# The last FFN stage with half of its tokens sorted by expert through DRAM

## What is computed

```
x = x + 0.5 * _L1_ffn_ref(_layernorm(x), ...)
shared = silu(xf @ shared_w1.T) * (xf @ shared_w2.T) @ shared_w3.T
scores = sigmoid(xf @ router_w.T)
_, top_idx = top_k(scores + expert_bias, 2)
gates = scores * one_hot(top_idx, 8).sum(-2)
h = silu(h1) * h2 * gates[:, :, None]        # h1, h2 of all 8 experts
routed = einsum('teh,edh->td', h, w3)
```

## Time and profile before

| | us |
|---|---|
| runs | 730.72, 729.73, 727.52 (median 729.73) |
| span of the profiled execution, first to last instruction | 725.0 |
| its own time | not among the three runs shown |
| PE busy | 676.2 (93%) |
| DVE busy | 570.1 (79%) |
| ACT busy | 419.2 (58%) |
| POOL busy | 325.0 (45%) |

### The profile page before, as it was taken

How to read it: one execution, slowest core, us unless ns; L and a number is a source line. 1 busy time by engine, 2 the same in 40 slices (tenths; PEclk the granted TensorE clock), 3 DMA queues, 4 the chain that set the end, 5 groups by cost and what they waited for, 6 DMA issues and landing times. The chain is left out here.

```text
span 725.0 us, 12469 instructions
## 1 busy us (share of the span) xinstructions
PE 676.2 (93%) x4100; PEld 505.7 (70%) x4100; DVE 570.1 (79%) x1308; ACT 419.2 (58%) x757; POOL 325.0 (45%) x404
## 2 busy tenths in 40 slices
PE   6899998797879999999999888999999997999997
PEld 5677774643457777777778676777777775777785
DVE  5799977899968888988989856666766675889774
ACT  4567686885245555556655657555565654555553
POOL 2668883201227766465658461220413200555463
PEclk9999999999999999999999989999999999999999
DMA  6625520000013232222222000000000000323141
GB/s 168 201 99 177 173 72 1 0 1 1 1 40 137 70 106 89 87 61 83 94 58 90 29 1 2 1 2 1 2 1 0 0 2 3 116 71 120 55 122 43
DMA packets 34329, 43.16 MB, mean 60 GB/s; under 512 B 5216, under 2 KB 17504, under 8 KB 34272
## 3 DMA queue, kind: packets, MB, share of 16 engines
q1 hardware_dynamic: 34272, 42.46, 18.9%
HBM read 41.13 MB, written 1.31 MB: 59 GB/s over the span
## 5 line engine op out<-in xcount | busy, mean ns | idle before, releaser
L698 POOL TENSOR_TENSOR p_prod<-p_p,p_gate_row 128x512 f32<-128x512 f32 x128 | 203.9, 1604 | 106.9 <-DVE p_p L505 62.4
L385 ACT ACTIVATE p_sil<-p_ps_a 128x512 f32<-128x512 f32 x176 | 105.3, 598 | 131.4 <-PE p_ps_a L100 128.3
L510 DVE TENSOR_TENSOR p_hlo<-p_prod,p_hhi 128x512 fp32r<-128x512 f32 x176 | 150.3, 855 | 0.3 <-ACT p_hhi L394 0.2
L505 DVE TENSOR_TENSOR p_p<-p_sil,p_ps_b 128x512 f32<-128x512 f32 x128 | 87.1, 681 | 52.6 <-ACT p_sil L385 38.1
L394 ACT CAST p_hhi<-p_prod 128x512 fp32r<-128x512 f32 x176 | 108.1, 615 | 23.0 <-POOL p_prod L698 22.9
L98 PE MATMUL p_ps_a<-xt_hi,w_uphi 128*128 128x512 f32 x176 | 74.2, 422 | 0.0
L98 PE MATMUL p_ps_acc<-p_hhi,w_downhi 128*128 128x512 f32 x176 | 71.1, 404 | 1.2 <-DVE p_hlo L510 1.0
L98 PE MATMUL p_ps_b<-xt_hi,w_uphi 128*128 128x512 f32 x176 | 71.0, 404 | 0.2
L99 PE MATMUL p_ps_a<-xt_lo,w_uphi 128*128 128x512 f32 x176 | 70.1, 399 | 0.0
L100 PE MATMUL p_ps_a<-xt_hi,w_uplo 128*128 128x512 f32 x176 | 70.1, 398 | 0.0
L100 PE MATMUL p_ps_b<-xt_hi,w_uplo 128*128 128x512 f32 x176 | 70.0, 398 | 0.0
(11 more groups left out here) (355 smaller groups left out, 1425.1 us busy)
## 6 DMA issues: line engine op xcount, KB each, us to landing
p_gate_row<-gate_rows SPq DMA_DIRECT2D x128, 256.0 KB, 3.3
w_rawbuf<-in_L_ffn_fc_w_dram SPq DMA_DIRECT2D x3, 512.0 KB, 7.1
w_rawbuf<-in_L_ffn_w_dram SPq DMA_DIRECT2D x3, 512.0 KB, 6.1
out_dram<-x SPq DMA_DIRECT2D x4, 256.0 KB, 3.6
w_rawbuf<-in_L_ffn_shared_w_dram SPq DMA_DIRECT2D x3, 256.0 KB, 5.6
x<-in_L_attn_x_dram SPq DMA_DIRECT2D x2, 256.0 KB, 3.9
x<-in_L_attn_x_dram SPq DMA_DIRECT2D x1, 512.0 KB, 9.3
mb_xraw<-in_L_attn_W_B_dram SPq DMA_DIRECT2D x1, 512.0 KB, 4.8
```

Source lines behind the costliest of these rows:

```text
L385: nc.scalar.activation(sil[:, u % 2], ps_a[:, u % 2], ACT.Silu).then_inc(c["sil"].sem, 1)
L505: nc.vector.tensor_tensor(dst, sil[:, u % 2], ps_b[:, u % 2], ALU.mult).then_inc(c["p1"].sem, 1)
L510: nc.vector.tensor_tensor(hlo[:, u % R], prod[:, u % R], hhi[:, u % R].bitcast(F32), ALU.subtract).then_inc(c["hlo"].sem, 1)
L698: G.tensor_tensor(prod[:, u % R], p1[:, u % 2], gate_row[:, e % ROWS], ALU.mult).then_inc(c["prod"].sem, 1)
```

## The change

Blocks 0 and 1 of the last stage (1024 tokens) keep only their 4 shared units; their 8 expert units go. Blocks 2 and 3 stay dense with 12 units. So the stream (`sparse_stream`) has 4 + 4 + 12 + 12 = 32 units for 48. For the 1024 tokens the kernel instead:

1. routes both blocks at the start (`z_route`, `z_choose`), counts with 9 small matmuls (`z_rank`) where each of the 2048 (token, expert) pairs stands in a list sorted by expert, each expert padded to whole tiles: 23 slot tiles at most (`z_places`),
2. scatters each normalised token to its two slots in DRAM: 16 indirect DMAs on POOL,
3. in six groups of four slot tiles (the last of three), between unit 15 and unit 16: loads the rows, turns them, and multiplies each tile with the weights of its own expert alone, which a register read from SBUF picks (`value_load`, 23 times on PE),
4. stores the results in DRAM, fetches each token's two rows with 16 indirect DMAs on POOL, and adds them, weighed by the gate, on DVE (`z_add`).

In block 3 the gate is multiplied by DVE and no longer by POOL. The slots are zeroed beforehand by one DMA of 128 x 23 x 128 numbers, put ahead of `load_rest`. Mamba keeps the normalised tokens of both blocks (one copy per block on POOL, `save_head`).

The diff, cut to its core:

```diff
+def three_pass_turned(pe, out, tokens, weights):
+    pe.matmul(out, tokens[0], weights[0], start=True, stop=False)
+    pe.matmul(out, tokens[0], weights[1], start=False, stop=False)
+    return pe.matmul(out, tokens[1], weights[0], start=False, stop=True)
...
+                G.memset(consts["zeros"], 0.0)
...
+def sparse_stream(nc, tag, counts, sb, ps, x, xt, consts, kind, gate_dram, rows_dram, results_dram, norm, kept_xn, le, tail, out_dram, room, spent_zs, spent_raw):
+    LEAD, BEHIND, RING, ROWS = 4, 2, 4, EXPERTS
+    S, U, w = kind.shared, kind.units, kind.w
+    FIRST = (0, S, 2 * S, 2 * S + U)
+    UNITS = 2 * S + 2 * U
+    CUT = 16
+    GROUPS = -(-SLOT_TILES // BT)
+    HALF = 2 * BT
+    STRIDE = P
...
+        @block.tensor
+        def _(pe):
...
+            def z_rank():
+                pe.wait_ge(c["z_both"].sem, c["z_both"].at(1))
+                pe.matmul(ranks, le[:], z_both[:], start=True, stop=False)
+                for j in range(1, HALF + 1):
+                    last = pe.matmul(ranks[:, j:], z_ones[:], z_both[:, 0:HALF + 1 - j], start=False, stop=j == HALF)
+                last.then_inc(c["z_rank"].sem, 1)
+            def z_owners(s):
+                if s == 0:
+                    pe.wait_ge(c["z_owner"].sem, c["z_owner"].at(1))
+                for q in range(s * BT, s * BT + sizes(s)):
+                    owner[q] = pe.value_load(z_owner[0:1, q:q + 1], min_val=0, max_val=(EXPERTS - 1) * STRIDE)
+            def z_turn_x(s):
+                row = c[f"z_row{s % 2}"]
+                pe.wait_ge(row.sem, row.at(16 * (s // 2 + 1)))
+                if s == 0:
+                    pe.wait_ge(c["gts"].sem, c["gts"].at(2))
+                else:
+                    pe.wait_ge(c["z_xlo"].sem, c["z_xlo"].at(s))
+                for t in range(sizes(s)):
+                    last = pe.transpose(ps_t[:, bass.ts(t, P)], z_rows[s % 2][:, t], ident[:])
+                last.then_inc(c["z_xt"].sem, 1)
+            def z_up(s):
+                if s < 2:
+                    before = c[("sil", "p1")[s]]
+                    pe.wait_ge(before.sem, before.at(CUT + LEAD))
+                else:
+                    pe.wait_ge(c["z_h"].sem, c["z_h"].at(s - 1))
+                pe.wait_ge(c["z_xlo"].sem, c["z_xlo"].at(s + 1))
+                for t in range(sizes(s)):
+                    some = bass.ds(owner[s * BT + t] * 2 + S * 2 * P, 2 * P)
+                    last = three_pass_turned(pe, raised(s)[:, t].rearrange("p a c -> p (a c)"),
+                                             [q[s % 2][:, bass.ts(t, P)] for q in (z_xhi, z_xlo)], [q[:, some] for q in up_flat])
+                last.then_inc(c["z_up"].sem, 1)
+            def z_turn_h(s):
+                pe.wait_ge(c["z_h"].sem, c["z_h"].at(s + 1))
+                if s:
+                    pe.wait_ge(c["z_hlo"].sem, c["z_hlo"].at(s))
+                else:
+                    pe.wait_ge(c["out"].sem, c["out"].at(2))
+                for t in range(sizes(s)):
+                    last = pe.transpose(ps_o[:, bass.ts(t, P)], z_h[s % 2][:, t], ident[:])
+                last.then_inc(c["z_ht"].sem, 1)
+            def z_down(s):
+                pe.wait_ge(c["z_hlo"].sem, c["z_hlo"].at(s + 1))
+                if s:
+                    pe.wait_ge(c["z_yc"].sem, c["z_yc"].at(s))
+                else:
+                    pe.wait_ge(c["lgs"].sem, c["lgs"].at(2))
+                for t in range(sizes(s)):
+                    some = bass.ds(owner[s * BT + t] + S * P, P)
+                    last = three_pass_turned(pe, ps_l[:, bass.ts(t, P)], [q[s % 2][:, bass.ts(t, P)] for q in (z_hhi, z_hlo)],
+                                             [q[:, some] for q in down_flat])
+                last.then_inc(c["z_y"].sem, 1)
...
+            def step(g):
+                if g + LEAD < UNITS:
+                    up(g + LEAD)
+                if g == 0:
+                    z_rank()
+                if g in (4, 8, 20):
+                    turn_out(block_of(g) - 1)
+                down(g)
+                if g == 1:
+                    turn_x(2)
+                if g == 2:
+                    route(2)
+                if g == 3:
+                    turn_logits(2)
+                if g == 5:
+                    turn_gates(2)
+                if g == 6:
+                    turn_x(3)
+                if g == 8:
+                    route(3)
+                if g == 9:
+                    turn_logits(3)
+                if g == 12:
+                    turn_gates(3)
+                if g == 14:
+                    z_turn_x(0)
+                    z_owners(0)
+                if g == 15:
+                    z_turn_x(1)
+                    z_owners(1)
+            z_route(0, ps_l)
+            z_route(1, ps_acc)
+            up(0)
+            z_turn_logits()
+            tail.to_tokens(pe, -1, last_bank)
+            up(1)
+            tail.turn_y(pe, -1, last_bank)
+            up(2)
+            up(3)
+            tail.project_out(pe, -1, last_bank)
+            for g in range(CUT):
+                step(g)
+            for s in range(GROUPS):
+                z_up(s)
+                if s:
+                    z_turn_h(s - 1)
+                if s >= 2:
+                    z_down(s - 2)
+                if s + 2 < GROUPS:
+                    z_turn_x(s + 2)
+                    z_owners(s + 2)
+            step(CUT)
+            z_turn_h(GROUPS - 1)
+            z_down(GROUPS - 2)
+            step(CUT + 1)
+            z_down(GROUPS - 1)
+            for g in range(CUT + 2, UNITS):
+                step(g)
+            turn_out(NBLK - 1)
...
+        @block.vector
+        def _(dve):
+            def weigh(g):
+                if is_shared(g) or block_of(g) < NBLK - 1:
+                    return
+                row = row_of(expert(g))
+                dve.wait_ge(row.sem, row.at(16 * (block_of(g) - 1)))
+                dve.wait_ge(c["p1"].sem, c["p1"].at(g + 1))
+                dve.wait_ge(c["hlo"].sem, c["hlo"].at(g + 1 - RING))
+                dve.wait_ge(c["prod"].sem, c["prod"].at(at_expert(g)))
+                V.tensor_tensor(prod[:, g % RING], p1[:, g % 2], gate_row[:, expert(g)], ALU.mult).then_inc(c["prod"].sem, 1)
...
+            def z_add(j):
+                dve.wait_ge(c[f"z_back{j}"].sem, c[f"z_back{j}"].at(32))
+                if j == 0:
+                    dve.wait_ge(c["z_gate"].sem, c["z_gate"].at(1))
+                for k in range(2):
+                    V.scalar_tensor_tensor(out=x[:, j], in0=z_back[j][k], scalar=z_gate[:, k, j:j + 1], in1=x[:, j],
+                                           op0=ALU.mult, op1=ALU.add).then_inc(c["z_add"].sem, 1)
+                    dve.wait_ge(c["z_add"].sem, c["z_add"].at(2 * j + k + 1))
+            def step(g):
+                if g + LEAD < UNITS:
+                    gated(g + LEAD)
+                    weigh(g + LEAD)
+                if g + BEHIND < UNITS:
+                    low(g + BEHIND)
+                if g in (4, 8, 20):
+                    add_out(block_of(g) - 1)
+                if g == 0:
+                    z_places()
+                if g == 1:
+                    low_x(2)
+                    z_owners()
+                if g == 2:
+                    measure(3)
+                if g == 4:
+                    choose(2)
+                if g == 5:
+                    normal(3)
+                if g == 6:
+                    low_x(3)
+                if g == 7:
+                    z_gates()
+                if g == 10:
+                    choose(3)
+                if g == 14:
+                    z_low_x(0)
+                if g == 15:
+                    z_low_x(1)
+                if g >= 24:
+                    z_add(g - 24)
+            measure(2)
+            z_choose()
+            gated(0)
+            normal(2)
+            tail.gated(dve, -1, BATCH - 1, last_bank)
+            gated(1)
+            tail.low_y(dve, -1, last_bank)
+            gated(2)
+            low(0)
+            tail.add_out(dve, -1, BATCH - 1, last_bank)
+            gated(3)
+            low(1)
+            for g in range(CUT):
+                step(g)
+            for s in range(GROUPS):
+                z_mul(s)
+                if s:
+                    z_low_h(s - 1)
+                if s + 2 < GROUPS:
+                    z_low_x(s + 2)
+            step(CUT)
...
+        @block.gpsimd
+        def _(pool):
+            def scatter(j):
+                for k in range(2):
+                    G.indirect_dma_start(rows_dram[:, :], bass.IndirectOffsetOnAxis(ap=z_place[:, k, j:j + 1], axis=0),
+                                         kept_xn[:, j], None).then_inc(c["z_scat"].sem, 16)
+            def gather(j):
+                for k in range(2):
+                    G.indirect_dma_start(z_back[j][k], None, results_dram[:, :],
+                                         bass.IndirectOffsetOnAxis(ap=z_place[:, k, j:j + 1], axis=0)).then_inc(c[f"z_back{j}"].sem, 16)
```

(60 more changed lines are left out.)

486 lines of the change are left out of this document (478 added, 8 removed).

## The result

The changed kernel takes 746.68 us (median of 4 runs, 744.06 to 748.79), the kernel before 729.38 in the same session: a ratio of 1.0242, 95% interval 1.0207 to 1.0277. It is slower by 17.3 us, where I had forecast 5 us, with half of the chance on a slower kernel.

A forecast was written before the change was run, and what follows sets the result against it. PE was taken to set the pace of the last stage, with DVE having 13% to spare. PE's -11.4 us and waits summed to +5.1 on the span of 725.0; with 4.7 outside it, rounded to 734.5 us, range 721 to 749.

The forecast's parts named there:

- PE alone: Last stage, PE work only: 33.8 us of expert units go, 22.4 of small matmuls and turns come, -11.4 us.
- Item 1: Head of the last stage: two blocks are routed before the first product, so PE waits for DVE, +3.0 us.
- Item 2: Scatters on POOL stand before the gates of block 2, for which PE waits, +3.5 us.
- Item 3: Register reads on PE in the six sorted groups, 0.75 us each with checks, three quarters hidden, +4.5 us.
- the 744 by that price: Alternative estimate: register reads at 0.6 us each, 13.8 us if nothing hides, in place of 4.5; about 744 us.
- Item 4: Zeroing of the slots, issued ahead of the weights, delays the gate rows of block 2 in stage 0, +2.7 us.
- Item 5: Gate rows of block 3, queued behind the last `z_keep`, make DVE wait after the sorted part, +1.0 us.
- Item 6: DVE's extra work in block 3, +0.5 us; last sums and stores at the end, +1.0; Mamba's copy, +0.3.
- Outside the span: Time outside the profiled span: 4.7 us, added to the forecast span of 730.1 to give 734.8.
- Rival C: DVE and POOL block each other at the ten early scatters: 6.9 us more at item 2, 741.4 us; chance 0.13.
- Rival B: PE's register reads are bare, 1.2 us each with checks: 27.6 us in place of 4.5, 748 us; chance 0.12.
- Rival A: Faster: the lead of `up`, four units ahead of `down`, covers the waits in the last stage, 722.8 us; chance 0.32.

The follow-up runs named there:

- fillers: Changed kernel plus forty matmuls with unread results, placed where PE waits for Mamba's tail and the gates of blocks 2 and 3: 741.88 us.
- together: Changed kernel with all moves at once: reads spread, Mamba's tail first, fill late, gates of blocks 2 and 3 earlier, block 3's rows and weighs moved: 733.36 us.
- rows3_early: Changed kernel with SP sending the gate rows of block 3 right after the load of group 4, ahead of the result stores: 747.55 us.
- no_gather: Changed kernel without the 16 gathers and the 16 gated sums on DVE: 742.37 us.
- second profile: The unchanged kernel before, run and profiled once more: span 727.7 us.

## Why the prediction was wrong

The sign was right and the mechanism mostly: less work on PE, given back as waits in PE's order. The size was not, 5 us against 17. Two steps failed: each wait was priced at its length alone, without the low clock behind it (4.8 us for three waits), and the gates of block 3 had no term at all (2.65 us, and 1.6 of that clock). Items 3 and 6 were sized too small besides.

- **PE alone, -11.4.** The cadences held: three passes of a tile take 0.36 us up and 0.335 down, as 3 x 0.12 and 3 x 0.11. About 1.7 us that are missing beside the named waits I did not assign.
- **Item 1, +3.0, found 4.4.** The choice took 3.0 us, as figured (615.12 to 618.11). I left out `normal(2)`, 1.05 us, as a term of its own although I named it, and the clock behind the wait.
- **Item 2, +3.5, found 4.42 in the wait.** Price (1.26 against 1.2) and count were right. The 1.7 that would stay with free scatters no run shows; the choice of block 2 was ready at 642.18 and its gates take POOL 0.66, which makes about 1.1 after PE's arrival at 641.78. The step ended at the wait; the nine matmuls behind it cost 1.9 more.
- **The missing step: the clock behind a wait.** I had read 0.57 at 607 to 611 and used it only to describe the head. The rows already hinted at what I didn't draw, that a wait costs more than its length; here the three long ones cost a third to 0.6 of it again (1.3 for 4.12, 1.9 for 4.42, 1.6 for 2.65). `fillers` shows 4.8 us for three waits. This is the largest error.
- **The missing term: gates of block 3.** `weights(3)` stands behind the fourth `weigh` of block 2 on POOL, and that one waits for DVE's product behind the choice of block 3. 2.65 us and the clock; the wait stays 2.63 to 2.65 in each variant that keeps this order and puts nothing in its place, and none is left in `together`, which makes these gates one `weigh` earlier and turns them one step later. I followed POOL's queue to the gates of block 2 and no further.
- **Item 3, +4.5, found 6.9.** I took 0.75 us a read with three quarters hidden; it is 0.45 with two thirds bare (6.9 of 23 x 0.45 = 10.4). The Trainium skill (DMA: Bandwidth & Descriptors, Latency and other measured facts) has about 600 ns as the least that a `tensor_load` takes; the trace here has 0.298 for one as the median of 23, and the gaps give 0.45 with the checks, so the measurement decides, and the 744 by that price came nearer to the result only by other errors.
- **Item 4, +2.7, found 1.2 by medians that don't tell it from nothing.** The fill landed in 7.5 us, near the 9 that I took; PE's wait behind it was 0.58 us, so the lead of `weigh` hid nearly all.
- **Item 5, +1.0.** The gap came (1.72), but it was no independent term: `rows3_early` shows that DVE and SP's queue give it back.
- **Item 6, +1.5, found 2.6 to 4.3.** I costed the sums one step at a time (units 24 and 25) and not as 16 x 0.37 = 5.9 us on an engine already at 1.98 of 2.1 us (722.45 to 724.43) for all of block 3. `no_gather` gives 4.3 by the medians and 2.6 by the stage; the gaps and the slow end in the profile make 3.7.
- **Outside the span** I took 4.7 us and got 1.7; and the span of 725.0 that the sum was made against was 2.7 below the second profile. These two nearly cancel.

Rival C, the ports: ten early scatters, seven at 0.95 or 0.96 us and three at 1.25, 1.10 and 1.36, while DVE was busy 11.82 of 15 us (631 to 646), leave no room for 6.9 us. By the rule of the Trainium skill (SBUF — State Buffer, SBUF: two separate sides) POOL cannot write its descriptors while DVE runs an operation of a two-port mode; if any of the operations here was one, at most 0.4 us of such a lock can be seen in one scatter. Where POOL computes, there is more to see: DVE's L1362 took 1.29 us at 661.92, while a `weigh` ran on POOL until 663.15, against 0.18 at 640.43. Rival B was near in time by luck: most reads are bare, as it said, but they cost 7 us and not 27. Rival A is refuted: the lead of four units hid no wait that stands in PE's own order.

## What to carry to other kernels

Price a wait of an in-order engine by its length and by what follows it: here the waits of 1.87, 2.65, 4.12 and 4.42 us were all followed by matmuls at half the clock, and filling three of them with matmuls whose result nobody reads won 4.8 us, although it was added work. When a helper engine's queue is put in a new order, follow it to its end and ask of each item what stands ahead of it and what that waits for. Put register reads where long operations are queued. Before an engine that is busy 95% of the time is given small work at the end of a program, add all of it up.
